# Two of four casts moved from VectorE to ScalarE, with reordered steps, in a fused recurrent-and-feed-forward kernel

## The chip, the cores and the metric

The kernel runs on one core of one Trainium2 chip. The metric is the device time of one execution in microseconds; of several runs the median is taken. Times inside an execution come from a profile of one run and count from the start of its span.

## The reference

The input x has 8 sequences of 512 positions with 128 features, in float32. Three residual stages follow each other:

```
x = x + 0.5 * ffn(layernorm(x))
x = x + attn(layernorm(x))
x = x + 0.5 * ffn(layernorm(x))      # the same weights as the first
ffn:  h = silu(x @ w1.T * s1) * (x @ w2.T * s2)       # 128 -> 512
      h = gelu(h @ h1.T * s3); h = gelu(h @ h2.T * s4) # 512 -> 512, twice
      return h @ w3.T * s5                             # 512 -> 128
attn: h_t = tanh(x_t @ B + h_(t-1) @ A.T)              # 16 states, along the sequence
      y = h @ C;  return y @ W_out.T + b_out
```

The middle stage is a scan along the 512 positions. The kernel cuts each sequence into 8 blocks of 64 positions, starts every block from a guess, and repeats the scan if the block ends disagree.

## The kernel before

**Tiles and turns.** The work is cut into 8 chunks of 512 columns (N), features or hidden units on the 128 partitions. Each chunk goes through the feed-forward stage twice, so there are 16 turns, g = 0 to 15. One turn computes, for its chunk, layer 2, layer 3 and layer 4 and, for the next chunk, layer 1. Layer 1 gives the product y1, layers 2 and 3 give y2 and y3, each with four tiles m = 0 to 3 of 128 hidden units. There are five kinds of turns: the first (g = 0), `early_turn` (g = 1 to 5), `middle_turn` (g = 6 to 8), `turn` with a next chunk (g = 9 to 14) and the last one (g = 15).

**Exactness.** Every activation is split in a high part, which is the value cast to the reduced type that TensorE multiplies, and a low part, value minus high part. Each product is then two matmuls of 128x128 by 512, one with each part (L256). The high part is made by a cast or, for y2 and y3, by a second Gelu straight from the accumulator (L1022, after L1019 has made the full value). The low part is a subtraction, on VectorE (`low`, L702) or on GpSimd (L1249).

**Layer 1 in pieces.** For each tile m, ScalarE makes tanh of the first product (`layer1`, th, L1001), VectorE makes u from it (`gate`, L675) and y1 from u and the second product (`gated`, L685), and VectorE then casts y1 into y1_hi (`y1_high`, L692). For chunk 0 alone ScalarE casts y1 (L1006). GpSimd makes y1_lo of tiles 0 to 2, VectorE that of tile 3. One semaphore, y1_hi_r, counts all casts: tile m of chunk g is there at 4g + m + 1.

**The scan.** It goes beside the feed-forward work, eight steps in a turn. One step is a chain over three engines: TensorE multiplies the last state by A (a matmul with 32 columns, L388), ScalarE makes two tanh of 32 columns (L1038, L1039), and VectorE subtracts to get the mixed state h (`scan_low`, L721). TensorE's next step waits for that. The first pass of the scan goes in turns 2 to 6, the second in turns 6 to 13.

**Order.** Every engine has one queue in program order, and the order of all work on it is written out by hand in the turn functions. A wait holds all that is behind it on its engine. TensorE's order in a turn is layer 2 of tiles 0 to 3 (with layer 4 of the chunk before, the attention product and the front transposes set into tile 0), layer 1 of the next chunk's tiles 0 and 1, layer 3 of tile 0, layer 1 of tile 2, layer 3 of tiles 1 and 2, layer 1 of tile 3, layer 3 of tile 3, with `scan_step` set between. In early turns steps 3, 6 and 7 stand in front of layer 1 tile 0, layer 3 tile 2 and layer 1 tile 3. In middle turns the second-pass steps stand two to a tile of layer 3.

**Normalisation.** In early turns the chunk g + 2 is normalised with tokens on the partitions: VectorE takes statistics (`first_stats`) and the negated mean (`mean_negated`, nmean), GpSimd makes the inverse deviation (rs_f, L1244) and the bias (nbias, L1259), and ScalarE applies them in four instructions of 128 columns (`normalise`, L1056). Chunk `mid` = g - 1 is normalised for the scan on VectorE, after `middle_stats`. From turn 7 on, the front of the next chunk comes from the attention result: VectorE adds the residual into lnin (L729), TensorE transposes it (`front_tokens`, L274), VectorE takes statistics.

The lines that ScalarE runs in an early turn, and VectorE's order around the casts:

```
gelu2(g, 1, lambda: step(1))
normalise(g + 2)
step(2)
...
gate(g, 0); step(at[0]); gated(g, 0); gate(g, 1); y1_high(g, 0); step(at[1])
gated(g, 1); step(at[2]); y1_high(g, 1); gate(g, 2); step(at[3])
gated(g, 2); step(at[4]); y1_high(g, 2)
```

Of the kernel before, what the change touches and what calls it, by code (L numbers as in the profile page):

```python
# [35 lines left out]
CHUNKS = 8  # L36
# [20 lines left out]
def build(nc, xT, xtok, w1T, w2T, h1T, h2T, w3T, scales, Ablk, Brep, CTrep, WoutT, ident_d, mask_d, outT):  # L57
    with ExitStack() as ctx:
# [129 lines left out]
        th_r = sem("th_r")  # L188
        u_r = sem("u_r")
        y1_r = sem("y1_r")  # L190
        y1_hi_r = sem("y1_hi_r")
        y1_lo_pool = sem("y1_lo_pool")
        y1_lo_dve = sem("y1_lo_dve")
        l2_mm = sem("l2_mm")
# [56 lines left out]
        def _(pe):  # L251
# [71 lines left out]
            def layer2(g, m, gen, beside=lambda k: None):  # L323
                if m == 0:
                    pe.wait_ge(y1_r, 4 * g + 3)
                if m == 1:
                    wait(pe, y3_hi_r, 4 * g)
                if m == 2:
                    wait(pe, l4_out, g)
                for k in range(KT):  # L330
                    if m == 0:
                        pe.wait_ge(y1_hi_r, 4 * g + k + 1)
                        if k < KT - 1:
                            pe.wait_ge(y1_lo_pool, (KT - 1) * g + k + 1)
# [96 lines left out]
            def first_layer2(m, ks, gen, high=True, finish=False):  # L431

                for k in ks:
                    if high:
                        pe.wait_ge(y1_hi_r, k + 1)
                        if k < KT - 1:
                            pe.wait_ge(y1_lo_pool, k + 1)
                        else:
                            pe.wait_ge(y1_lo_dve, 1)
                    mm = split_mm(B2[m][:, :], 2, k, m, y1_hi[:, k, :], y1_lo[:, k, :], high and k == 0,  # L440
                                  finish and k == KT - 1, gen, high)
                if finish:
                    mm.then_inc(l2_mm, 1)
# [183 lines left out]
        def _(dve):  # L627
# [61 lines left out]
            def y1_high(g, m):  # L689
                dve.wait_ge(y1_r, 4 * g + m + 1)  # L690
                wait(dve, l2_mm, 4 * g)
                nc.vector.tensor_copy(y1_hi[:, m, :], y1[:, m, :]).then_inc(y1_hi_r, 1)  # L692

            def layer1(g, m, late=False):
                gate(g, m, late)
                gated(g, m, late)
                if not late and not (isinstance(g, int) and g == 0):
                    y1_high(g, m)

            def low(g, k, hi_r, y, y_hi, y_lo, out_sem):  # L700
                dve.wait_ge(hi_r, 4 * g + k + 1)
# [51 lines left out]
            def first_gates(g, step, at):  # L753

                gate(g, 0)
                step(at[0])
                gated(g, 0)
                gate(g, 1)
                y1_high(g, 0)
                step(at[1])  # L760
                gated(g, 1)
                step(at[2])
                y1_high(g, 1)
                gate(g, 2)
                step(at[3])
                gated(g, 2)
                step(at[4])
                y1_high(g, 2)

            def end_turn(g):  # L770

                gated(g + 1, KT - 1)
                y1_high(g + 1, KT - 1)
                low(g + 1, KT - 1, y1_hi_r, y1, y1_hi, y1_lo, y1_lo_dve)
                low(g, 3, y3_hi_r, y23, y3_hi, y3_lo, y3_lo_dve)

            def early_turn(g, mid, scan):
                def step(t):
                    if scan is not None and t is not None:
                        scan_low(scan, t)  # L780
                xn_low(g + 1)
                layer4(0, g - 1, g - 1)
                step(0)
                first_stats(g + 2)
                middle_stats(mid)
                mean_negated(g + 2)
                step(1)
                low(g, 1, y2_hi_r, y23, y2_hi, y2_lo, y2_lo_dve)
                step(2)
                normalise("m", mid, MI, mv_m, rs_m, xnt_m)  # L790
                step(3)
                low(g, 3, y2_hi_r, y23, y2_hi, y2_lo, y2_lo_dve)
                first_gates(g + 1, step, (4, None, 5, None, None))
                step(6)
                low(g, 1, y3_hi_r, y23, y3_hi, y3_lo, y3_lo_dve)
                step(7)
                low(g, 2, y3_hi_r, y23, y3_hi, y3_lo, y3_lo_dve)
                gate(g + 1, KT - 1)
                end_turn(g)

            def middle_turn(g, c):
# [31 lines left out]
                    xn_low(g + 1)  # L833
                    normalise("m", mid, MI, mv_m, rs_m, xnt_m)
                low(g, 3, y2_hi_r, y23, y2_hi, y2_lo, y2_lo_dve)
                first_gates(g + 1, step, (None, 0, 1, 2, 3))
                step(4)
                low(g, 1, y3_hi_r, y23, y3_hi, y3_lo, y3_lo_dve)
                step(5)
# [6 lines left out]
            def turn(k, g, att, scan, joined=True):  # L846
# [19 lines left out]
                step(3)  # L866
                low(g, 3, y2_hi_r, y23, y2_hi, y2_lo, y2_lo_dve)
                if not last:
                    first_gates(g + 1, step, (4, None, 5, None, None))
                step(6)  # L870
                low(g, 1, y3_hi_r, y23, y3_hi, y3_lo, y3_lo_dve)
                step(7)
# [50 lines left out]
            nc.vector.tensor_scalar(general[:, :], F[4][0:1, 0:1], 0.0, None, ALU.is_gt).then_inc(gen_ready, 1)  # L923

            xn_low(1)
            low(0, KT - 1, y1_hi_r, y1, y1_hi, y1_lo, y1_lo_dve)
            first_stats(2)
            mean_negated(2)
            low(0, 1, y2_hi_r, y23, y2_hi, y2_lo, y2_lo_dve)
            low(0, 3, y2_hi_r, y23, y2_hi, y2_lo, y2_lo_dve)  # L930
            for m in range(KT - 1):
                layer1(1, m)
            low(0, 1, y3_hi_r, y23, y3_hi, y3_lo, y3_lo_dve)
            low(0, 2, y3_hi_r, y23, y3_hi, y3_lo, y3_lo_dve)
            layer1(1, KT - 1)
            low(0, 3, y3_hi_r, y23, y3_hi, y3_lo, y3_lo_dve)
            low(1, KT - 1, y1_hi_r, y1, y1_hi, y1_lo, y1_lo_dve)
            early_turn(1, 0, None)
            early_turn(2, 1, 0)
            with dve.Fori(3, FIRST_PASS + 1) as k:  # L940
# [4 lines left out]
            def round_(r):  # L945
                gb = r * CHUNKS
                if isinstance(r, int):
                    middle_turn(CHUNKS, 2)
                else:
                    restart(r)  # L950
                    for t in range(CSTEPS):
                        scan_low(gb + FIRST_PASS, t)
                    attention(gb, 0)
                    front_stats(gb + CHUNKS)
                    normalise("f", gb + CHUNKS, FR, mv_f, rs_f, xnt_f)
                    for t in range(CSTEPS):
                        scan_low(gb + FIRST_PASS + 1, t)
                    xn_low(gb + CHUNKS)
                    attention(gb + 1, 1)
                    for m in range(KT):  # L960
                        layer1(gb + CHUNKS, m, late=True)
                    low(gb + CHUNKS, KT - 1, y1_hi_r, y1, y1_hi, y1_lo, y1_lo_dve)
                    turn(0, gb + CHUNKS, None, gb + FIRST_PASS + 2, False)
                turn(1, gb + 1 + CHUNKS, (gb + 2, 2), gb + FIRST_PASS + 3)
                with dve.Fori(2, CHUNKS - 2) as k:
# [25 lines left out]
        def _(act):  # L991
# [11 lines left out]
            def y1_high(g, m):  # L1003
                act.wait_ge(y1_r, 4 * g + m + 1)
                wait(act, l2_mm, 4 * g)
                nc.scalar.copy(y1_hi[:, m, :], y1[:, m, :]).then_inc(y1_hi_r, 1)  # L1006

            def layer1_late(g, beside=lambda m: None):
                for m in range(KT):
# [39 lines left out]
                act.wait_ge(step_h, n * CSTEPS)  # L1049
                nc.scalar.copy(SC[:, 0:HCOLS], cols(xb_all, c, HCOLS)).then_inc(sc_set, 1)  # L1050

            def normalise(g):
                act.wait_ge(nbias_r, g)
                wait(act, feat["f"], g)
                for q in range(QT):
                    i = nc.scalar.activation(xnt_f[:, q * P:(q + 1) * P], cols(xt_all, g)[:, q * P:(q + 1) * P],  # L1056
                                             ACT.Identity, bias=nbias[:, q:q + 1], scale=rs_f[:, q:q + 1])
                i.then_inc(normed["f"], 1)

            def early_turn(g, mid, scan):  # L1060
# [3 lines left out]
                step(0)  # L1064
                gelu2(g, 0)
                gelu2(g, 1, lambda: step(1))
                normalise(g + 2)
                step(2)
                gelu2(g, 2)
                step(3)  # L1070
                gelu2(g, 3)
# [3 lines left out]
                middle_copy(mid)  # L1075
                step(5)
                gelu3(g, 0, lambda: layer1(g + 1, 2))
                step(6)
                gelu3(g, 1)
                step(7)  # L1080
                gelu3(g, 2)
                layer1(g + 1, 3)
                gelu3(g, 3)
                front(g + 2)
                keep_xb(mid)

            def middle_turn(g, c):
                mid = g - 1
# [18 lines left out]
                middle_copy(mid)  # L1107
                keep_xb(mid)
                step(0)
                gelu3(g, 0, lambda: layer1(g + 1, 2))  # L1110
                step(1)
                step(2)
                step(3)
                gelu3(g, 1, lambda: step(4))
                step(5)
                gelu3(g, 2, lambda: step(6))
                layer1(g + 1, 3)
                step(7)
# [2 lines left out]
            def turn(g, nxt, scan):  # L1121
# [16 lines left out]
                step(4)  # L1138
                step(5)
                gelu3(g, 0, lambda: layer1(g + 1, 2) if nxt else None)  # L1140
                step(6)
                gelu3(g, 1)
                step(7)
                gelu3(g, 2)
                if nxt:
# [47 lines left out]
            gelu2(0, 3)  # L1193
            layer1(1, 1)
            layer1(1, 2)
            gelu3(0, 0)
            gelu3(0, 1)
            gelu3(0, 2)
            layer1(1, 3)
            gelu3(0, 3)  # L1200
# [37 lines left out]
        def _(pool):  # L1238
            def inverse_std(kind, g, mv, ve, rs):
# [3 lines left out]
                wait(pool, normed[kind], g)  # L1243
                pool.tensor_tensor(rs[:, :], ve[:, :], mhalf[:, :], ALU.pow).then_inc(rstd[kind], 1)  # L1244

            def low(g, k, hi_r, per, y, y_hi, y_lo, out_sem, free):
                pool.wait_ge(hi_r, 4 * g + k + 1)
                wait(pool, *free)
# [1 line left out]

            def layer1(g, ms=range(KT - 1)):
                for m in ms:
                    low(g, m, y1_hi_r, 4, y1, y1_hi, y1_lo, y1_lo_pool, (l2_mm, 4 * g))

            def bias(g):
                pool.wait_ge(rstd["f"], g + 1)
# [162 lines left out]
```

## Time and profile before

| What | Value |
|---|---|
| runs | 426.45, 427.07, 427.39 us; median 427.07 |
| profiled execution | 425.79 us |
| its span | 424.0 us, of which 1.8 us lie outside |
| TensorE matmuls busy | 392.3 us, 93% |
| VectorE busy | 298.5 us, 70% |
| ScalarE busy | 254.8 us, 60% |
| GpSimd busy | 165.8 us, 39% |
| TensorE clock granted over the span | 0.979 |

A busy share is the time in which an engine ran instructions, over the span. TensorE's matmuls overlap in the record, so a matmul that shows 0.40 us can be followed by the next after 0.23 us. A share of 93% says that TensorE sets the time in most places, and that the places where it stands are what other engines can give back.

### The profile page before, as it was taken

What the parts mean: (1) busy time and instruction counts of PE and PEld (TensorE: products, weight loads), DVE (VectorE), ACT (ScalarE), POOL (GpSimd) and SP (SyncE); (2) the same over time, 40 slices, a digit from 0 to 9 for tenths busy, and PEclk for the clock granted to TensorE, in tenths of its full rate; (3) what the DMA queues carried; (4) which work ended last, traced back from release to release, by engine and by line L of the source; (5) the groups of instructions that cost most, each with busy time, mean ns of one, the idle gap of its engine ahead of it and who ended that gap; (6) DMA issues with size and microseconds to landing.
All of it is one profiled execution on the core that took longest, in us unless ns stands there. A gap on an engine that the chain in (4) does not pass through costs nothing.

```text
span 424.0 us, 6711 instructions
## 1 busy us (share of the span) xinstructions
PE 392.3 (93%) x1787; PEld 301.2 (71%) x1787; DVE 298.5 (70%) x756; ACT 254.8 (60%) x609; POOL 165.8 (39%) x156
## 2 busy tenths in 40 slices
PE   6868999999999999998989989999999999999981
PEld 4655877777777777776767767777877777777760
DVE  4694869687676859577787876878678685877511
ACT  3547576575758657676555666656565766656550
POOL 3334455461535535153351533525233353525120
PEclk9698999999999999999999999999999999999996
DMA  7900000000000000000101001010100001010001
GB/s 256 424 16 2 1 26 0 26 2 25 2 1 25 0 25 0 25 2 1 49 2 49 2 0 52 1 49 2 49 0 25 25 0 49 0 50 2 25 1 32
DMA packets 6078, 14.02 MB, mean 33 GB/s; under 512 B 1056, under 2 KB 1568, under 8 KB 5792
## 3 DMA queue, kind: packets, MB, share of 16 engines
q1 hardware_dynamic: 5040, 13.37, 8.2%
q10 hardware_dynamic: 1008, 0.29, 0.3%
q8 instruction: 13, 0.21, 0.2%
q14 instruction: 17, 0.14, 0.1%
HBM read 7.37 MB, written 2.10 MB: 22 GB/s over the span
## 4 chain that ended last, share of the span: by engine, by line
PE 52%; issue 16%; DVE 15%; ACT 10%; POOL 3%; DMA 1%; DVEq 1%; ACTq 0%; POOLq 0%
PE F L256 44%; DVE u L675 5%; DVE y L685 3%; ACT th L1001 2%; ACT y_hi L1022 2%; ACT xnt_f L1056 2%; PE FR L284 2%; ACT y L1019 2%; DVE xnt_f L663 1%; POOL rs_f L1244 1%; DVE y_hi L692 1%; PE SC L373 1%; DVE st_f L630 1%; PE SC L388 1%; DVE h L721 1%
## 5 line engine op out<-in xcount | busy, mean ns | idle before, releaser
L256 PE MATMUL F<-y_hi,w_hi 128*128 128x512 f32 x512 | 211.9, 414 | 7.4 <-DVE y_lo L702 2.5
L256 PE MATMUL F<-y_lo,w_hi 128*128 128x512 f32 x512 | 203.0, 396 | 0.0
L1249 POOL TENSOR_TENSOR y_lo<-y,y_hi 128x512 fp32r<-128x512 f32 x96 | 130.2, 1363 | 105.7 <-DVE y_hi L692 60.2
L256 PEld LDWEIGHTS F<-y_hi,w_hi 128*128 128x128 f32 x512 | 96.5, 189 | 33.9 <-issue 5.9
L256 PEld LDWEIGHTS F<-y_lo,w_hi 128*128 128x128 f32 x512 | 96.8, 189 | 18.4
L1019 ACT ACTIVATE y<-F,sc 128x512 f32<-128x512 f32 x112 | 76.5, 683 | 51.2 <-PE F L256 51.2
L702 DVE TENSOR_TENSOR y_lo<-y,y_hi 128x512 fp32r<-128x512 f32 x96 | 68.8, 729 | 44.4 <-ACT y_hi L1022 44.0
L1022 ACT ACTIVATE y_hi<-F,sc 128x512 fp32r<-128x512 f32 x112 | 76.4, 682 | 0.0
L1038 ACT ACTIVATE h<-SC 128x32 fp32r<-128x32 f32 x104 | 20.3, 195 | 77.2 <-PE SC L388 77.2
L256 PE MATMUL F<-xn_hi,w_hi 128*128 128x512 f32 x119 | 50.7, 426 | 2.2 <-POOL w_lo L1295 1.9
L1241 POOL TENSOR_TENSOR ve_f<-mv_f,epsc 128x4 f32<-128x4 f32 x16 | 3.2, 200 | 114.1 <-DVE mv_f L635 108.8
L256 PE MATMUL F<-xn_lo,w_hi 128*128 128x512 f32 x119 | 47.2, 396 | 0.0
L692 DVE CAST y_hi<-y 128x512 fp32r<-128x512 f32 x60 | 45.6, 760 | 1.1
L1001 ACT ACTIVATE th<-F,s1h 128x512 f32<-128x512 f32 x61 | 40.7, 688 | 7.4 <-PE F L256 5.2
L685 DVE SCALAR_TENSOR_TENSOR y<-F,s12h,u 128x512 f32<-128x512 f32 x58 | 43.4, 748 | 1.8
L675 DVE SCALAR_TENSOR_TENSOR u<-th,F 128x512 f32<-128x512 f32 x61 | 41.4, 678 | 2.2 <-ACT th L1001 2.2
L721 DVE TENSOR_TENSOR h<-SC,h 64x32 fp32r<-64x32 f32 x104 | 18.4, 177 | 29.8 <-ACT SC L1039 29.0
L388 PEld LDWEIGHTS SC<-h,a_mix 128*128 128x128 f32 x103 | 19.3, 187 | 21.1 <-DVE h L721 17.7
L256 PEld LDWEIGHTS F<-xn_hi,w_hi 128*128 128x128 f32 x119 | 22.6, 190 | 8.8 <-ACT w_hi L1152 2.1
L388 PE MATMUL SC<-h,a_mix 128*128 128x32 f32 x103 | 20.9, 203 | 8.3 <-DVE h L721 8.3
L256 PE MATMUL FR<-y_hi,w_hi 128*128 128x512 f32 x64 | 26.0, 406 | 0.6 <-DVE y L685 0.6
L256 PE MATMUL FR<-y_lo,w_hi 128*128 128x512 f32 x64 | 25.3, 395 | 0.0
(121 smaller groups left out, 359.0 us busy)
## 6 DMA issues: line engine op xcount, KB each, us to landing
x_all<-in_xT SPq DMA_DIRECT2D x1, 2048.0 KB, 16.7
x_all<-x1c SPq DMA_DIRECT2D x8, 256.0 KB, 2.3
x_all<-lnin SPq DMA_DIRECT2D x8, 256.0 KB, 2.3
out<-outb SPq DMA_DIRECT2D x8, 256.0 KB, 2.1
x_all<-in_xtok SPq DMA_DIRECT2D x1, 1536.0 KB, 12.5
w_raw<-in_h1T SPq DMA_DIRECT2D x2, 512.0 KB, 7.7
w_raw<-in_h2T SPq DMA_DIRECT2D x2, 512.0 KB, 9.5
x_all<-in_xtok SPq DMA_DIRECT2D x2, 256.0 KB, 4.6
```

The costliest lines, as they stand in the source:

```text
L256: mm = nc.tensor.matmul(out, wtile(w, layer, k, m), y, start=first and i == 0, stop=last and i == len(pairs) - 1)
L388: nc.tensor.matmul(SC[:, span(t)], a_mix[:, :], states, start=False, stop=True, skip_group_check=True).then_inc(step_mm, 1)
L675: nc.vector.scalar_tensor_tensor(out=u[:, m % 2, :], in0=th[:, m % 2, :], scalar=1.0, in1=l1_banks(g, m, late)[0][:, :], op0=ALU.add, op1= ...
L685: nc.vector.scalar_tensor_tensor(out=y1[:, m, :], in0=l1_banks(g, m, late)[1][:, :], scalar=s12h[:, m:m + 1], in1=u[:, m % 2, :], op0=ALU. ...
L692: nc.vector.tensor_copy(y1_hi[:, m, :], y1[:, m, :]).then_inc(y1_hi_r, 1)
L702: nc.vector.tensor_tensor(y_lo[:, k, :], y[:, k, :], y_hi[:, k, :].bitcast(F32), ALU.subtract).then_inc(out_sem, 1)
L721: nc.vector.tensor_tensor(h[0:64, span(t)], SC[0:64, span(CSTEPS + t)], h[0:64, span(t)].bitcast(F32), ALU.subtract).then_inc(step_h, 1)
L1001: nc.scalar.activation(th[:, m % 2, :], l1_banks(g, m, late)[0][:, :], ACT.Tanh, scale=s1h[:, m:m + 1]).then_inc(th_r, 1)
L1019: nc.scalar.activation(y23[:, m, :], bankt[:, :], ACT.Gelu, scale=s)
L1022: nc.scalar.activation(y_hi[:, m, :], bankt[:, :], ACT.Gelu, scale=s).then_inc(hi_r, 1)
L1038: nc.scalar.activation(h[:, span(t)], SC[:, span(t)], ACT.Tanh)
L1249: pool.tensor_tensor(y_lo[:, k, :], y[:, k, :], y_hi[:, k, :].bitcast(F32), ALU.subtract).then_inc(out_sem, 1)
```

## The change

ScalarE takes over the casts of y1's tiles 1 and 2 for every chunk from 1 on; tiles 0 and 3 stay on VectorE. Since two engines now cast, each tile gets a semaphore of its own, y1_hi_r[m], and the waits on TensorE, VectorE and GpSimd name the tile. In early turns scan step 2 on ScalarE goes between the second and the third of the four `normalise` instructions, and the negated mean goes ahead of `middle_stats` on VectorE. In middle turns scan step 1 on ScalarE goes ahead of the tanh of tile 2, and a cast stands behind step 2 and another behind step 5. No matmul, no DMA and no arithmetic is added or removed.

```diff
-        y1_hi_r = sem("y1_hi_r")
+        y1_hi_r = [sem(f"y1_hi_r{m}") for m in range(KT)]
...
-                        pe.wait_ge(y1_hi_r, 4 * g + k + 1)
+                        pe.wait_ge(y1_hi_r[k], g + 1)
...
             def layer1(g, m, late=False):            # VectorE
                 gate(g, m, late)
                 gated(g, m, late)
-                if not late and not (isinstance(g, int) and g == 0):
-                    y1_high(g, m)
+
+            def low1(g):
+                dve.wait_ge(y1_hi_r[KT - 1], g + 1)
+                nc.vector.tensor_tensor(y1_lo[:, KT - 1, :], y1[:, KT - 1, :], y1_hi[:, KT - 1, :].bitcast(F32),
+                                        ALU.subtract).then_inc(y1_lo_dve, 1)
...
                 gated(g, 1)                           # VectorE, first_gates
                 step(at[2])
-                y1_high(g, 1)
                 gate(g, 2)
                 step(at[3])
                 gated(g, 2)
-                step(at[4])
-                y1_high(g, 2)
...
                 first_stats(g + 2)                    # VectorE, early_turn
+                mean_negated(g + 2)
                 middle_stats(mid)
-                mean_negated(g + 2)
...
-            def normalise(g):                         # ScalarE
+            def normalise(g, between=lambda: None):
                 act.wait_ge(nbias_r, g)
                 wait(act, feat["f"], g)
                 for q in range(QT):
+                    if q == QT // 2:
+                        between()
...
-                normalise(g + 2)                      # ScalarE, early_turn
-                step(2)
+                normalise(g + 2, lambda: step(2))
...
                 gelu3(g, 0, lambda: layer1(g + 1, 2))
+                y1_high(g + 1, 1)
                 step(6)
                 gelu3(g, 1)
+                y1_high(g + 1, 2)
                 step(7)
...
+            def first_and_gate(g, step):
+                step(1)
+                layer1(g + 1, 2)
...
                 step(0)                               # ScalarE, middle_turn
-                gelu3(g, 0, lambda: layer1(g + 1, 2))
-                step(1)
+                gelu3(g, 0, lambda: first_and_gate(g, step))
                 step(2)
+                y1_high(g + 1, 1)
                 step(3)
                 gelu3(g, 1, lambda: step(4))
                 step(5)
+                y1_high(g + 1, 2)
                 gelu3(g, 2, lambda: step(6))
...
                 gelu3(g, 0, lambda: layer1(g + 1, 2) if nxt else None)   # ScalarE, turn
+                if nxt:
+                    y1_high(g + 1, 1)
                 step(6)
                 gelu3(g, 1)
+                if nxt:
+                    y1_high(g + 1, 2)
                 step(7)
```

In `middle_turn` and `turn` VectorE's order stays as it was without the two casts. The first turn gets the same two casts on ScalarE, between the two Gelus of layer 3 tiles 0 and 1. GpSimd's `low1` is the same subtraction as before with the tile's own semaphore.

## Rows read from the trace of the kernel before

**Rows 1.** Waits: engine and line, whom it waited for; total us, times, longest.
```profile
PE SC L388 <- DVE h L721: 8.3, 19, 0.7
```
**Rows 2.** Timeline of TensorE, early turn 5: start, us, instruction, idle before.
```profile
158.18 0.40 PE L256 MATMUL F<-y_lo,w_hi 128*128 128x512 f32 x1
...
159.35 0.50 PE L256 MATMUL F<-xn_hi,w_hi 128*128 128x512 f32 x1
...
163.68 0.48 PE L256 MATMUL F<-xn_hi,w_hi 128*128 128x512 f32 x1
...
166.55 0.18 PE L388 MATMUL SC<-h,a_mix 128*128 128x32 f32 x1
166.77 0.50 PE L256 MATMUL F<-y_hi,w_hi 128*128 128x512 f32 x1
...
168.50 0.40 PE L256 MATMUL F<-y_lo,w_hi 128*128 128x512 f32 x1
...
169.40 0.47 PE L256 MATMUL F<-xn_hi,w_hi 128*128 128x512 f32 x1
```
**Rows 3.** Timeline of GpSimd, ScalarE and VectorE in early turn 5, normalisation and first gate.
```profile
154.52 1.01 POOL L1244 TENSOR_TENSOR rs_f<-ve_f,mhalf 128x4 f32<-128x4 f32 x1 [0.16 <-POOL ve_f L1241]
156.15 0.61 POOL L1259 TENSOR_TENSOR nbias<-nmean,rs_f 128x4 f32<-128x4 f32 x1 [0.62 <-POOL rs_f L1244]
...
156.99 1.65 ACT L1056 ACTIVATE xnt_f<-x_all,nbias,rs_f 128x128 f32 x4 [1.27 <-POOL nbias L1259]
...
162.78 0.75 DVE L685 SCALAR_TENSOR_TENSOR y<-F,s12h,u 128x512 f32<-128x512 f32 x1
```
**Rows 4.** Timeline of GpSimd, VectorE and ScalarE in early turn 5, around the cast of tile 2.
```profile
166.22 2.54 POOL L1249 TENSOR_TENSOR y_lo<-y,y_hi 128x512 fp32r<-128x512 f32 x2 [0.39 <-ACT y_hi L1022]
...
167.62 1.43 DVE L692 CAST y_hi<-y 128x512 fp32r<-128x512 f32 x1
...
167.53 0.68 ACT L1022 ACTIVATE y_hi<-FR,sc 128x512 fp32r<-128x512 f32 x1
```
**Rows 5.** The two cast lines by source: count, shortest/median/longest ns, first and last start.
```profile
L692 DVE CAST y_hi<-y x60: 408/428/1503, 40.6 to 394.6; 128x512 fp32r<-128x512 f32 x60
L1006 ACT CAST y_hi<-y x4: 617/623/627, 17.3 to 26.5; 128x512 fp32r<-128x512 f32 x4
```
**Rows 6.** Timeline of TensorE and VectorE, middle turn 7 and opening of turn 8.
```profile
217.12 0.40 PE L256 MATMUL FR<-y_lo,w_hi 128*128 128x512 f32 x1
...
218.33 0.48 PE L256 MATMUL FR<-y_hi,w_hi 128*128 128x512 f32 x1
...
219.12 0.40 PE L256 MATMUL FR<-y_lo,w_hi 128*128 128x512 f32 x1
...
220.30 0.48 PE L256 MATMUL F<-y_hi,w_hi 128*128 128x512 f32 x1
...
228.36 0.75 DVE L729 SCALAR_TENSOR_TENSOR lnin<-MI,sc,x_all 128x512 f32<-128x512 f32 x1
...
229.16 0.66 PE L274 MATMUL FR<-ident,lnin 128*128 128x128 f32 x4
```
**Rows 7.** Timeline of TensorE and VectorE, turn 11 and opening of turn 12.
```profile
317.44 0.18 PE L388 MATMUL SC<-h,a_mix 128*128 128x32 f32 x1
317.73 0.50 PE L256 MATMUL F<-y_hi,w_hi 128*128 128x512 f32 x1
...
319.46 0.40 PE L256 MATMUL F<-y_lo,w_hi 128*128 128x512 f32 x1
...
320.28 0.48 PE L256 MATMUL F<-xn_hi,w_hi 128*128 128x512 f32 x1
...
325.63 0.74 DVE L729 SCALAR_TENSOR_TENSOR lnin<-MI,sc,x_all 128x512 f32<-128x512 f32 x1
...
326.70 0.65 PE L274 MATMUL FR<-ident,lnin 128*128 128x128 f32 x4
```
**Rows 8.** Timeline of TensorE in early turn 1, which has no scan.
```profile
60.70 0.50 PE L256 MATMUL F<-xn_hi,w_hi 128*128 128x512 f32 x1 [0.27 <-ACT y_hi L1022]
```

More of the change, by code:

```diff
@@ L434, in first_layer2 @@
                     if high:
-                        pe.wait_ge(y1_hi_r, k + 1)
+                        pe.wait_ge(y1_hi_r[k], 1)
                         if k < KT - 1:
@@ L691, in y1_high @@
                 wait(dve, l2_mm, 4 * g)
-                nc.vector.tensor_copy(y1_hi[:, m, :], y1[:, m, :]).then_inc(y1_hi_r, 1)
+                nc.vector.tensor_copy(y1_hi[:, m, :], y1[:, m, :]).then_inc(y1_hi_r[m], 1)
             def layer1(g, m, late=False):
@@ L773, in end_turn @@
                 y1_high(g + 1, KT - 1)
-                low(g + 1, KT - 1, y1_hi_r, y1, y1_hi, y1_lo, y1_lo_dve)
+                low1(g + 1)
                 low(g, 3, y3_hi_r, y23, y3_hi, y3_lo, y3_lo_dve)
@@ L792, in early_turn @@
                 low(g, 3, y2_hi_r, y23, y2_hi, y2_lo, y2_lo_dve)
-                first_gates(g + 1, step, (4, None, 5, None, None))
+                first_gates(g + 1, step, (4, None, 5, None))
                 step(6)
@@ L835, in middle_turn @@
                 low(g, 3, y2_hi_r, y23, y2_hi, y2_lo, y2_lo_dve)
-                first_gates(g + 1, step, (None, 0, 1, 2, 3))
+                first_gates(g + 1, step, (None, 0, 1, 2))
+                step(3)
                 step(4)
@@ L868, in turn @@
                 if not last:
-                    first_gates(g + 1, step, (4, None, 5, None, None))
+                    first_gates(g + 1, step, (4, None, 5, None))
                 step(6)
@@ L925, in _ @@
             xn_low(1)
-            low(0, KT - 1, y1_hi_r, y1, y1_hi, y1_lo, y1_lo_dve)
+            low1(0)
             first_stats(2)
@@ L932, in _ @@
                 layer1(1, m)
+                if m == 0:
+                    y1_high(1, 0)
             low(0, 1, y3_hi_r, y23, y3_hi, y3_lo, y3_lo_dve)
@@ L935, in _ @@
             layer1(1, KT - 1)
+            y1_high(1, KT - 1)
             low(0, 3, y3_hi_r, y23, y3_hi, y3_lo, y3_lo_dve)
-            low(1, KT - 1, y1_hi_r, y1, y1_hi, y1_lo, y1_lo_dve)
+            low1(1)
             early_turn(1, 0, None)
@@ L961, in round_ @@
                         layer1(gb + CHUNKS, m, late=True)
-                    low(gb + CHUNKS, KT - 1, y1_hi_r, y1, y1_hi, y1_lo, y1_lo_dve)
+                    low1(gb + CHUNKS)
                     turn(0, gb + CHUNKS, None, gb + FIRST_PASS + 2, False)
@@ L1005, in y1_high @@
                 wait(act, l2_mm, 4 * g)
-                nc.scalar.copy(y1_hi[:, m, :], y1[:, m, :]).then_inc(y1_hi_r, 1)
+                nc.scalar.copy(y1_hi[:, m, :], y1[:, m, :]).then_inc(y1_hi_r[m], 1)
             def layer1_late(g, beside=lambda m: None):
@@ L1195, in _ @@
             layer1(1, 2)
-            gelu3(0, 0)
-            gelu3(0, 1)
+            gelu3(0, 0, lambda: y1_high(1, 1))
+            gelu3(0, 1, lambda: y1_high(1, 2))
             gelu3(0, 2)
@@ L1244, in inverse_std, with low1 @@
                 pool.tensor_tensor(rs[:, :], ve[:, :], mhalf[:, :], ALU.pow).then_inc(rstd[kind], 1)
+            def low1(g, m):
+                pool.wait_ge(y1_hi_r[m], g + 1)
+                wait(pool, l2_mm, 4 * g)
+                pool.tensor_tensor(y1_lo[:, m, :], y1[:, m, :], y1_hi[:, m, :].bitcast(F32),
+                                   ALU.subtract).then_inc(y1_lo_pool, 1)
             def low(g, k, hi_r, per, y, y_hi, y_lo, out_sem, free):
@@ L1252, in layer1 @@
                 for m in ms:
-                    low(g, m, y1_hi_r, 4, y1, y1_hi, y1_lo, y1_lo_pool, (l2_mm, 4 * g))
+                    low1(g, m)
             def bias(g):
```

## The prediction

> **What bounds the kernel now.** I read the waits first, then TensorE's timeline turn by turn, then the other engines around each gap. The first part of the page has TensorE nearly always busy, so time can only come from places where it stands. The largest wait of its matmuls after the start is for VectorE's scan state: 8.3 us in 19 waits [rows 1]. They fall two to a scanning early turn (g = 2 to 5), two to a middle turn (6 to 8), one to each of turns 9 to 13.
>
> The idle figure is less than what a gap costs, so I count from start to start. Between the first matmul of layer 1 tile 2 and scan step 6 of turn 5 lie 12 large matmuls in 2.87 us, 0.24 us each [rows 2]; a scan matmul that waits for nothing adds 0.03 us. What exceeds 0.24 or 0.27 us is a gap. Early turn 5 has three [rows 2]: 1.17 - 0.27 = 0.90 us at step 3, 0.22 - 0.03 = 0.19 us behind step 6, 0.90 - 0.27 = 0.63 us at step 7. A middle turn has two, 1.21 - 0.27 = 0.94 us at step 2 and 1.18 - 0.27 = 0.91 us at step 4 [rows 6]. A late turn has 0.29 - 0.03 = 0.26 us behind step 6 and 0.82 - 0.27 = 0.55 us at step 7 [rows 7].
>
> Two causes stand behind them. VectorE's cast takes 0.43 us alone, but up to 1.50 us [rows 5]. The long ones are those beside GpSimd: GpSimd's pair of subtractions ends at 168.76 us, and the cast that began at 167.62 us ends at 169.05 us, 0.29 us later [rows 4]. The cast stood until GpSimd was through, and scan steps and the gate of tile 2 stood behind it. The other cause is ScalarE: step 2 of an early turn waits behind a normalisation of 1.65 us, which itself began late because the bias waited for the negated mean [rows 3], and step 1 of a middle turn waits behind a tanh and a Gelu of tile 0.
>
> **The change part by part.**
>
> Casts. VectorE loses 30 of its 60 casts, ScalarE gets 30 of about 0.62 us [rows 5]. On VectorE the cast of tile 1 stood ahead of the gate of tile 2, that of tile 2 ahead of step 6 (early and late turns). Both leave the path, so the gap behind step 6 and the gap at step 7 close. On ScalarE the casts stand in front of steps 6 and 7. In turn 5 y1 of tile 2 is complete by 167.62 us, when the old cast begins, and ScalarE is busy with the Gelu of tile 1 until 168.21 us [rows 4], so the cast does not wait for its input. The step behind it starts when TensorE's matmul arrives, which is about when the cast ends; I cost it at nothing there, at most 0.62 us of delay for whoever is next on ScalarE.
>
> Semaphores per tile. The same waits with other names, no instruction more: nothing, in either direction, since each wait asks for the same cast as before.
>
> Negated mean first. VectorE stands before the middle statistics anyway, so this one short instruction of four columns is covered by TensorE's transposes. The bias then follows rs_f: it waited 0.62 us, and a hand-over inside GpSimd takes 0.16 us [rows 3]; it starts 0.46 us earlier. If the bias were not what ScalarE waits for, the gain would be 0; it is named as the releaser, so I take 0.46 (ends 0 and 0.62).
>
> Step 2 between halves. It begins behind 0.82 us of normalisation instead of 1.65 us, so with the bias it is 1.29 us earlier, more than the 0.90 us of the gap at step 3: that wait is gone. What is late next is the rest of ScalarE's queue. The Gelus of tiles 2 and 3 come only 0.46 us earlier, and through them VectorE's y1 of tile 0, for which TensorE's layer 1 tile 2 waits. That y1 ends at 163.53 us, TensorE starts at 163.68 us [rows 2, 3]; with 0.05 us of hand-over (as lnin to transpose, [rows 6]) 0.10 us are spare. So of the 0.90 us, 0.46 + 0.10 = 0.56 us can be kept, and I take 0.55.
>
> Early turns 2 to 5: 0.55 + 0.19 + 0.63 = 1.37 us each, 5.5 us (ends: 0.90 in place of 0.55 gives 6.9; 0.10 gives 3.7). Turn 1 has no scan, but TensorE waits there for a Gelu behind the same normalisation [rows 8]; 0.5 us, and 0.26 us as behind step 6: 0.76 us (0.27 to 0.9). The first turn has its casts where TensorE waits for tile 1's y1 itself: nothing.
>
> Middle turns. ScalarE's step 1 no longer waits for tanh and Gelu, so step 2 on TensorE comes in time. VectorE's step 3 stood behind the gate of tile 2, which stood behind a long cast; without it step 4 is in time. I walked the order through with the durations of the rows: tanh, Gelu and cast now stand between steps 1, 2 and 3 on ScalarE, and about 0.05 us is lost there. The larger debt comes due in the next turn. ScalarE has 1.24 us more to do between the third-layer Gelus, VectorE's gate of tile 3 falls back by about 0.34 us against TensorE, and VectorE is then busy without a break until lnin. lnin ends at 229.11 us and the transpose starts at 229.16 us [rows 6], nothing spare. So 0.94 + 0.91 - 0.05 - 0.34 = 1.46 us each, 4.4 us for three (ends: 1.85, and 0.6 if both casts are due in full, hence 5.6 and 1.8).
>
> Turns 9 to 13: 0.26 + 0.55 = 0.81 us. The same debt arises, because VectorE's subtraction of tile 2 now meets GpSimd's last one, but here at most 326.70 - 0.05 - 326.37 = 0.28 us are spare at the transpose [rows 7]. Lateness I estimate as in the middle turns, 0.34 to 0.4 us, of which 0.10 us is left: 0.71 us each, 3.55 us for five (ends 4.05 and 1.0). Turn 14 has no scan and keeps 0.26 us.
>
> Sum: 5.5 + 0.76 + 4.4 + 3.55 + 0.26 = 14.5 us. The profiled execution took 425.79 us, so 411.3 us; it lies 1.28 us under the median of the runs, so the median goes from 427.07 to 412.6 us. All gaps closed without debt would be 17.5 us, 409.5 us.
>
> A rule speaks against the move. The row shows the cast at 0.43 us on VectorE alone and 0.62 us on ScalarE [rows 5], so ScalarE is dearer wherever GpSimd is quiet. The Trainium skill (Perfetto Trace Analysis, Optimizing Scalar/DVE Operations) says that an operation which has a VectorE performance mode is faster there, and that moving it to ScalarE may make sense if VectorE is saturated. VectorE is at 70% and not saturated. By that rule 30 casts would each cost about 0.2 us more, some 6 us if all lie on the path, and eat two fifths of the gain; the long casts of the row are what speaks for the move all the same.
>
> **The rivals.**
>
> *ScalarE becomes the link that is late.* Every cast lies in the queue between two scan steps. If the 0.19 us by which it is dearer is on the path in all 30 cases, that is 5.7 us: 412.6 + 5.7 = 418.3 us. Nearly the same comes out if in middle turns the four steps 1 to 4 are each 0.3 us late (3.6 us for three turns) and the early bias brings nothing (0.46 us in five turns, 2.3 us). For it: the queue of a middle turn has little air. Against it: ScalarE waited for TensorE's scan step in most places. The rule cited above points here. Chance 0.17.
>
> *Slower: ScalarE stands at the cast.* The queue is in order. If y1 of tile 2 came after the Gelu of tile 1, ScalarE would stand with step 7, two Gelus and the tanh of tile 3 behind it, and the opening of the next turn would be late. It decides from the point where the loss of a turn exceeds its gain, 14.5 / 14, about 1.0 us; the spare time in turn 5 is 168.21 - 167.62 = 0.6 us and grows since VectorE is relieved, so y1 would have to be 1.6 us later than now. If it were 2.1 us later, 0.5 us net in 14 turns give 434 us. The rows speak against it. Chance 0.05.
>
> *It does not do what it says.* The gaps close but TensorE waits as long somewhere else, the tiles' low parts for instance, which GpSimd now gets in another rhythm; 427 us. The low parts of tiles 1 and 2 are needed only in the next turn, which speaks against it. Chance 0.04.
>
> **How the numbers follow.** The forecast as summed has chance 0.74, with 409.5 to 416 us as its own range (the ends of the terms do not all fall together). About 0.2%, 0.9 us, is what a measurement of this kernel can tell from no change. The first rival is faster too, so faster has 0.74 + 0.17, and same and slower take 0.04 and 0.05. The range from 409.5 to 418.0 us takes in the forecast and a part of the first rival.
>
> **What would show it right or wrong.** In the profile after, the wait of L388 for VectorE falls from 8.3 us to under 2 us and from 19 to a few. Line 692 has 30 casts near 0.43 us and the casts on ScalarE are 34 at 0.62 us. Early turns fall by about 1.4 us, middle ones by 1.5, late ones by 0.7. In early turns layer 1 tile 2 shows a new small wait for y1, and behind middle turns the transpose of lnin shows one of 0.3 us. If the ScalarE casts took over 0.8 us, or if layer 2 waited for a low part of y1, the forecast would be wrong; if the wait of L388 stayed over 4 us, the first rival has it.

## The result and the profile after

The changed kernel takes 409.14 us (median of 4 runs, 408.61 to 409.59) against 426.76 us for the kernel before in the same comparison: a ratio of 0.960, 95% interval 0.958 to 0.963, or 17.6 us less. The forecast was 412.6 us, with a range from 409.5 to 418.0 us, worked out from a median of 427.07 us for the kernel before. The spans of the two profiled executions differ by 424.0 - 407.7 = 16.3 us.

First the head of the profile's page after, with the busy time of each engine, and the slices of TensorE:

```profile
span 407.7 us, 6683 instructions
PE 385.1 (94%) x1787; PEld 302.0 (74%) x1787; DVE 275.1 (67%) x726; ACT 270.4 (66%) x639; POOL 165.6 (41%) x156
...
PE   6868999999999999999999999999999999999980
```

VectorE lost 30 instructions and 23.4 us of busy time, ScalarE gained 30 and 15.6 us. TensorE ran the same 1787 matmuls. Next the two cast lines by source; they answer to [rows 5]:

```profile
L692 DVE CAST y_hi<-y x30: 411/426/429, 40.8 to 378.1; 128x512 fp32r<-128x512 f32 x30
L1010 ACT CAST y_hi<-y x34: 611/617/634, 17.5 to 373.6; 128x512 fp32r<-128x512 f32 x34
```

No cast on VectorE is long any more: the longest takes 429 ns instead of 1503. The waits of line 388, whose row before is [rows 1], show how little of the scan's hold is left. The matmul itself has no row any more, only its weight load. Here are the rows of ScalarE's wait for the scan matmul and of the weight load, first before, then after:

```profile
ACT h L1038 <- PE SC L388: 77.2, 76, 3.0
PEld SC L388 <- DVE h L721: 17.7, 24, 1.1
```

```profile
ACT h L1042 <- PE SC L388: 53.7, 53, 3.2
PEld SC L388 <- DVE h L724: 1.8, 8, 0.3
```

The time before TensorE's turns begin differs by up to 2.9 us from one profiled execution to the next, whatever the kernel. So I compare turns. A turn is taken from its opening transposes to those of the next, in us. Turns 1 to 7 go by those of L264, from turn 7 on by those of L274:

| From turn to turn | before | after | gain | forecast |
|---|---|---|---|---|
| 1 to 2 | 23.67 | 22.66 | 1.01 | 0.76 |
| 2 to 3 | 24.76 | 23.37 | 1.39 | 1.37 |
| 3 to 4 | 25.31 | 23.37 | 1.94 | 1.37 |
| 4 to 5 | 25.12 | 23.38 | 1.74 | 1.37 |
| 5 to 6 | 25.25 | 23.49 | 1.76 | 1.37 |
| 6 to 7 | 26.44 | 24.83 | 1.61 | 1.46 |
| 7 to 9, mean of two | 26.30 | 24.70 | 1.60 | 1.46 |
| 9 to 10 | 23.42 | 22.73 | 0.69 | 0.71 |
| 10 to 14, mean of four | 23.95 | 23.18 | 0.77 | 0.71 |

From the transposes of turn 1 to those of turn 14 it is 319.54 us before and 303.10 us after, 16.4 us less. This stretch is what I use to set the experiments beside each other. What follows it took 49.3 us before and 49.2 us after.

### The profile page after: what moved, and what is told of

Its sections match the earlier page's. It is cut to its first block, busy times and chain, and to the rows that moved or that the text cites. A ratio compares the mean times of both kernels' runs of the same rounds, so it can differ in the third digit from the quotient of the medians.

```text
span 407.7 us, 6683 instructions
## 1 busy us (share of the span) xinstructions
PE 385.1 (94%) x1787; PEld 302.0 (74%) x1787; DVE 275.1 (67%) x726; ACT 270.4 (66%) x639; POOL 165.6 (41%) x156
## 4 chain that ended last, share of the span: by engine, by line
PE 81%; DVE 7%; ACT 4%; issue 3%; POOL 2%; DMA 1%; DVEq 0%; POOLq 0%; ACTq 0%
PE F L256 67%; PE FR L256 8%; PE FR L284 2%; DVE xnt_f L663 1%; POOL rs_f L1260 1%; PE SC L373 1%; DVE st_f L630 1%; DVE u L675 1%; ACT y_hi L1026 1%; DVE y L685 1%; PE MI L284 1%; DMA x_all<-in_xtok 1%; PE MI L264 1%; ACT th L1005 1%; ACT y L1023 1%
## 5 line engine op out<-in xcount | busy, mean ns | idle before, releaser
L705 DVE TENSOR_TENSOR y_lo<-y,y_hi 128x512 fp32r<-128x512 f32 x80 | 65.0, 812 | 54.1 <-ACT y_hi L1026 54.1
L256 PEld LDWEIGHTS F<-xn_lo,w_hi 128*128 128x128 f32 x119 | 22.8, 191 | 3.5
L388 PEld LDWEIGHTS SC<-h,a_mix 128*128 128x128 f32 x103 | 19.3, 188 | 6.1 <-DVE h L724 1.8
```

The lines of the kernel that those rows point to most:

```text
L256: mm = nc.tensor.matmul(out, wtile(w, layer, k, m), y, start=first and i == 0, stop=last and i == len(pairs) - 1)
L388: nc.tensor.matmul(SC[:, span(t)], a_mix[:, :], states, start=False, stop=True, skip_group_check=True).then_inc(step_mm, 1)
L705: nc.vector.tensor_tensor(y_lo[:, k, :], y[:, k, :], y_hi[:, k, :].bitcast(F32), ALU.subtract).then_inc(out_sem, 1)
```

## Experiments

All are edits of the changed kernel. Each was measured against the kernel before on the same chip. The medians of the kernel before lay between 426.02 and 426.76 us.

**Casts only.** ScalarE casts, but no step is moved.

```diff
-                mean_negated(g + 2)
                 middle_stats(mid)
+                mean_negated(g + 2)
...
-                normalise(g + 2, lambda: step(2))
+                normalise(g + 2)
+                step(2)
...
-                gelu3(g, 0, lambda: first_and_gate(g, step))
+                gelu3(g, 0, lambda: layer1(g + 1, 2))
+                step(1)
                 step(2)
```

> Only the casts are moved; the negated mean, scan step 2 of early turns and scan step 1 of middle turns stand where they stood before. Theory A (the parts add up, gap by gap): the gaps behind step 6 and at step 7 close in early turns (0.19 + 0.63 us in four turns, 0.26 us in turn 1) and in late ones (0.8 us in five), and at step 4 in middle turns (0.9 us in three): about 10 us of the 17.6 us, 416.5 us. The gap at step 3 of early turns (0.9 us) and at step 2 of middle turns (0.94 us) stay. Theory B (the order is what counts, the casts only follow): under 5 us, above 421.5 us.

Measured: 415.04 us, ratio 0.973 (0.969 to 0.977); the stretch of turns took 309.44 us, 10.1 us less than before. That is theory A's figure. Late turns are as in the changed kernel (23.13 us). In early turns the wait behind step 6 and the one at step 7 are gone and the one at step 3 stays (0.79 us in turn 5, counted as in the prediction). In middle turns the gap at step 2 stays, as TensorE's timeline of turn 7 in this run shows (start, us, instruction, idle before):

```profile
212.62 0.40 PE L256 MATMUL FR<-y_lo,w_hi 128*128 128x512 f32 x1
213.70 0.28 PE L388 MATMUL SC<-h,a_mix 128*128 128x32 f32 x1 [0.68 <-DVE h L724]
213.83 0.48 PE L256 MATMUL FR<-y_hi,w_hi 128*128 128x512 f32 x1
```

From 212.62 to 213.83 us it is 1.21 us, the same as in [rows 6]. There is no second gap in the turn: with the cast off VectorE, step 4 is in time although step 2 is late.

**Order only.** The steps stay moved, VectorE casts in the old places.

```diff
                 gated(g, 1)
                 step(at[2])
+                y1_high(g, 1)
                 gate(g, 2)
                 step(at[3])
                 gated(g, 2)
+                step(at[4])
+                y1_high(g, 2)
```

(and the same two casts taken out of ScalarE's turns)

> All reordering is kept (negated mean, split normalisation, step 1 ahead of the tanh), but VectorE casts tiles 1 and 2 in their old places. Theory A: 0.9 us in four early turns, 0.5 us in turn 1, 0.94 us in three middle turns: about 7 us, 420 us; the long casts beside GpSimd and the gaps at step 7 remain. Theory B: 12 us or more, below 414.5 us.

Measured: 415.84 us, ratio 0.976 (0.972 to 0.980), the stretch 309.40 us, 10.1 us less. That is between the two theories, and 3 us more gain than A had. Late turns are as before within 0.07 us, early ones win 0.67 to 1.37 us. The difference to A's figure is in the middle turns. From turn 7 to turn 8 it took 24.54 us, less than the 24.70 us of the changed kernel, though VectorE still casts there. VectorE's and GpSimd's timelines of turn 7 show why:

```profile
207.95 0.17 DVE L724 TENSOR_TENSOR h<-SC,h 64x32 fp32r<-64x32 f32 x1
208.07 0.68 DVE L692 CAST y_hi<-y 128x512 fp32r<-128x512 f32 x1
208.66 0.68 DVE L675 SCALAR_TENSOR_TENSOR u<-th,F 128x512 f32<-128x512 f32 x1
...
207.16 1.29 POOL L1258 TENSOR_TENSOR y_lo<-y,y_hi 128x512 fp32r<-128x512 f32 x1 [2.94 <-DVE y_hi L692]
```

Scan step 1 comes earlier, so the cast of tile 1 starts 0.38 us before GpSimd's first subtraction ends (207.16 + 1.29 = 208.45 us) and takes 0.68 us, where it took 1.35 us in the kernel before. With the cast on VectorE, then, the gap at step 4 follows from the one at step 2; the casts-only run closes it the other way, by taking the cast off VectorE. Either edit is enough for that gap. The two sets of edits overlap: 10.1 + 10.1 = 20.2 us apart, 16.4 us together.

**Negated mean back** behind the middle statistics, all else as changed.

```diff
                 first_stats(g + 2)
-                mean_negated(g + 2)
                 middle_stats(mid)
+                mean_negated(g + 2)
```

> The changed kernel with the negated mean back behind the middle statistics. In the trace after, ScalarE starts to normalise 1.06 us sooner after the inverse deviation than before, not 0.46 us, because the bias also takes 0.20 us instead of 0.61 us. Theory A (the bias was held up by VectorE's subtraction of y2_lo at the shared port, besides starting late): the bias takes 0.6 us again, layer 1 waits in early turns, 0.8 us in four turns and 0.5 us in turn 1: 412.8 us. Rival (only the 0.46 us of the later start count): 0.35 us in five turns, 410.8 us.

Measured: 412.16 us, ratio 0.966 (0.962 to 0.970), the stretch 306.61 us. One short instruction in another place is worth 3.5 us, 0.7 us in each of turns 1 to 5. Here are GpSimd's and VectorE's rows of early turn 5 in this run, then GpSimd's and ScalarE's of the changed kernel:

```profile
150.80 1.01 POOL L1260 TENSOR_TENSOR rs_f<-ve_f,mhalf 128x4 f32<-128x4 f32 x1 [0.16 <-POOL ve_f L1257]
152.43 0.61 POOL L1281 TENSOR_TENSOR nbias<-nmean,rs_f 128x4 f32<-128x4 f32 x1 [0.63 <-POOL rs_f L1260]
...
152.16 0.14 DVE L653 TENSOR_SCALAR nmean<-mv_f 128x4 f32<-128x4 f32 x1
...
152.31 0.67 DVE L705 TENSOR_TENSOR y_lo<-y,y_hi 128x512 fp32r<-128x512 f32 x1
```

```profile
148.65 1.01 POOL L1260 TENSOR_TENSOR rs_f<-ve_f,mhalf 128x4 f32<-128x4 f32 x1 [0.16 <-DVE nmean L653]
149.74 0.20 POOL L1281 TENSOR_TENSOR nbias<-nmean,rs_f 128x4 f32<-128x4 f32 x1
...
150.06 0.88 ACT L1062 ACTIVATE xnt_f<-x_all,nbias,rs_f 128x128 f32 x2 [0.21 <-POOL nbias L1281]
```

With the mean late, the bias lands beside VectorE's subtraction of y2_lo and takes 0.61 us, until 153.04 us, 0.06 us after that subtraction ends (152.98 us). With the mean early it takes 0.20 us. That is so throughout: the median of the 7 instructions is 609 ns before and in this run, and 201 ns in the changed kernel. From the end of rs_f to the start of ScalarE's normalising it was 156.99 - 155.53 = 1.46 us before [rows 3], and is 150.06 - 149.66 = 0.40 us now.

TensorE's rows of early turn 5 in this run show where the time is lost:

```profile
154.47 0.39 PE L256 MATMUL F<-y_lo,w_hi 128*128 128x512 f32 x1
154.70 0.18 PE L388 MATMUL SC<-h,a_mix 128*128 128x32 f32 x1
154.76 0.49 PE L256 MATMUL F<-xn_hi,w_hi 128*128 128x512 f32 x1
...
155.55 0.40 PE L256 MATMUL F<-xn_lo,w_hi 128*128 128x512 f32 x1
156.18 0.50 PE L256 MATMUL F<-xn_hi,w_hi 128*128 128x512 f32 x1 [0.23 <-ACT y_hi L1026]
```

It is not lost at step 3: with the split and the late bias 0.29 us lie between the matmuls around the scan step, where 0.27 us is no gap. It is lost behind it: 156.18 - 155.55 - 0.24 = 0.39 us at layer 1 tile 1, which waits for a Gelu behind the late normalisation, and 159.77 - 159.33 - 0.27 = 0.17 us at layer 1 tile 2. The changed kernel has neither wait.

**No split.** Scan step 2 behind all four normalising instructions.

```diff
-                normalise(g + 2, lambda: step(2))
+                normalise(g + 2)
+                step(2)
```

> The changed kernel with scan step 2 behind all four normalising instructions. Theory A (with the early bias step 2 has time to spare: before it was due 0.9 us too late and it is now 1.06 us earlier): no difference, 409.1 us within 0.6. Rival (the split is needed): the gap at step 3 comes back with 0.4 us or more in four turns, 410.7 us or more.

Measured: 409.49 us, ratio 0.961 (0.957 to 0.965), the stretch 303.14 us against 303.10. The split is worth nothing once the bias is early. The run before shows the reverse for step 3: the split closes that gap also with a late bias. So either of the two closes it, but only the early bias brings the Gelus behind it in time.

**VectorE casts, but later** in its queue.

```diff
                 gate(g, 2)
+                y1_high(g, 1)
                 step(at[3])
                 gated(g, 2)
...
                 step(6)                               # step(4) in middle turns
+                y1_high(g + 1, 2)
                 low(g, 1, y3_hi_r, y23, y3_hi, y3_lo, y3_lo_dve)
```

(and ScalarE's two casts taken out of all turns)

> The changed kernel with the casts of tiles 1 and 2 on VectorE again, but not in their old places: that of tile 1 behind the gate of tile 2, that of tile 2 behind step 6 (behind step 4 in middle turns). Theory P (the place in VectorE's queue is what counted): the gaps stay closed and it takes 409 to 411 us. Theory L (the length counts too: a cast beside GpSimd's subtractions waits for the port and takes 1 to 1.5 us wherever it stands, and holds step 6 or the opening of the next turn): 0.3 to 0.7 us more in each of 9 early and late turns, 412 to 416 us.

Measured: 411.65 us, ratio 0.967 (0.963 to 0.971), the stretch 305.36 us, 2.3 us more than with ScalarE's casts. It lies between the theories. The place in the queue is worth most of it: early turns are as good as in the changed kernel but for one (3 to 4, 23.50 us), middle ones 0.1 us longer. Late turns take 23.46 us instead of 23.12 us, where VectorE's low parts of tiles 1 and 2, which stand in front of the residual add, take 1.53 and 1.24 us against 1.10 and 0.81 us in the same turn of the changed kernel:

```profile
304.70 1.53 DVE L705 TENSOR_TENSOR y_lo<-y,y_hi 128x512 fp32r<-128x512 f32 x1 [0.17 <-ACT y_hi L1030]
306.15 0.17 DVE L724 TENSOR_TENSOR h<-SC,h 64x32 fp32r<-64x32 f32 x1
306.69 1.24 DVE L705 TENSOR_TENSOR y_lo<-y,y_hi 128x512 fp32r<-128x512 f32 x1 [0.37 <-ACT y_hi L1030]
```

The length that theory L asked for did not come back: from turn 1 on one cast a turn is held up at all, and none takes more than 0.77 us, where up to two a turn took 0.96 to 1.50 us in the kernel before.

**Casts twice.**

```diff
+                if m in (1, 2) and not (isinstance(g, int) and g == 0):
+                    wait(act, dup_r, 2 * (g - 1))
+                    nc.scalar.copy(y1_dup[:, m - 1, :], y1[:, m, :]).then_inc(dup_r, 1)
                 nc.scalar.copy(y1_hi[:, m, :], y1[:, m, :]).then_inc(y1_hi_r[m], 1)
```

> The changed kernel with each of ScalarE's 30 casts done twice, first into a tile that nobody reads; the output is the same. Theory A (ScalarE has next to nothing spare behind the cast of tile 2, since VectorE's work up to lnin hangs on its next Gelu): two casts of 0.57 us more, about 0.9 us in each of turns 6 to 13 and little in early turns, where the opening has slack: 7 us more, 416 us. Rival (ScalarE, busy 66%, has room): under 2 us more, below 411 us.

Measured: 413.98 us, ratio 0.971 (0.968 to 0.975). The first cast of a pair takes 0.51 us from start to start, 30 of them 15 us, and 4.8 us of it show in the medians, 4.3 us in the stretch. Early turns do not change at all (23.37 and 23.38 us). From turn 7 to 8 it goes from 24.70 to 25.42 us, from 11 to 12 from 23.11 to 23.52 us. So theory A has the right turns and about one and a half times the size; ScalarE's spare time is neither none nor plenty, but differs by stage.

**Transposes later.**

```diff
-                if not last:
-                    to_features("f", xnt_f, FR, g + 1)
-                layer2(g, 3, gen)
+                layer2(g, 3, gen, lambda k: to_features("f", xnt_f, FR, g + 1) if k == 0 and not last else None)
```

> The changed kernel with one further step on TensorE in turns 9 to 14: the transposes back to features stand behind the first two matmuls of layer 2 tile 3 instead of ahead of them. In the trace after, they wait 0.37 us for VectorE's normalised tile in four turns. If that wait is covered by the two matmuls (0.47 us), layer 1 of the next chunk still has its input in time and it takes 1.5 us less than the changed kernel, 407.6 us. If ScalarE's copy and VectorE's low part behind the transposes are late for layer 1 instead, the same 409.1 us.

Measured: 409.34 us, ratio 0.961 (0.957 to 0.964). No gain; the wait only moved. TensorE's rows, first of the changed kernel at the transposes of turn 11, then of this run at layer 1 of the same turn:

```profile
293.82 0.18 PE L388 MATMUL SC<-h,a_mix 128*128 128x32 f32 x1
294.21 0.44 PE L284 MATMUL FR<-ident,xnt_f 128*128 128x128 f32 x2 [0.21 <-DVE xnt_f L663]
```

```profile
295.13 0.18 PE L388 MATMUL SC<-h,a_mix 128*128 128x32 f32 x1
295.55 0.49 PE L256 MATMUL F<-xn_hi,w_hi 128*128 128x512 f32 x1 [0.24 <-DVE xn_lo L668]
```

**Middle casts on VectorE**, in their old places, with the new order of steps.

```diff
                 step(at[2])
+                if cast:
+                    y1_high(g, 1)
                 gate(g, 2)
...
-                first_gates(g + 1, step, (None, 0, 1, 2))
+                first_gates(g + 1, step, (None, 0, 1, 2), True)
                 step(3)
+                y1_high(g + 1, 2)
                 step(4)
```

(and the same two casts taken out of ScalarE's middle turns)

> The changed kernel with the two casts of middle turns alone back on VectorE, in their old places; the order of steps is kept. In the run with order only a middle turn took 24.54 us from turn 7 to turn 8, in the changed kernel 24.70 us. If the order of steps alone closed the gaps of middle turns and ScalarE's casts cost something there: 0.16 us less in three turns, 408.6 us. If both are needed in middle turns: 2.7 us more, 411.8 us, as I forecast when I put the gap at step 4 down to the long cast.

Measured: 408.78 us, ratio 0.958 (0.953 to 0.962). A median of 0.4 us below the changed kernel is within the spread of the runs, but the turns are plain: 24.55 us from turn 7 to turn 8 instead of 24.70 us, the stretch 302.58 us instead of 303.10 us. The casts on ScalarE cost a little in middle turns, about 0.15 us a turn; that rests on the turns of the profiled executions, not on the medians.

**Statistics first** in turns 9 to 14.

```diff
-                if joined:
-                    layer4(1, g - 1, k - 1)
                 if not last:
                     front_stats(g + 1)
                 step(0)
+                if joined:
+                    layer4(1, g - 1, k - 1)
                 step(1)
```

> The changed kernel with VectorE's front statistics and scan step 0 of turns 9 to 14 ahead of the layer 4 output instead of behind it. The run with the transposes later showed that in these turns the chain from lnin over statistics, inverse deviation, normalising, transposes and low part to layer 1 is due 0.4 us too late wherever the transposes stand. The output of 0.75 us on VectorE stands in that chain. Theory A (this chain is the bound): the statistics start about 0.4 us sooner, the wait of 0.37 us at the transposes goes in five turns, 1.5 to 1.8 us less than the changed kernel, 407.5 us. Rival (layer 2 tile 2 then waits for the output that frees its accumulator): no gain, 409.1 us.

Measured: 407.73 us, ratio 0.956 (0.953 to 0.959), the stretch 302.01 us against 303.10. The wait for VectorE's tile is gone, and turns 10 to 13 take 22.84 us instead of 23.12 us, 13 to 14 takes 23.10 us instead of 23.35 us. The gain is 1.1 us, less than the 1.5 us expected: turn 9 to 10 did not change (22.72 us).

**Both of them.**

> The same with the casts of middle turns on VectorE as well. If the two gains are in different turns they add: 0.16 us in three turns more, 407.0 us; lower than every other kernel here.

Measured: 407.69 us, ratio 0.957 (0.955 to 0.959). In the stretch the gains add, 301.51 us; the medians do not tell this run from the one before it. Either is below the changed kernel by about 1.4 us, and below the kernel before by more than 18 us.

## Why the prediction was right, and where it was not

The direction and most of the size were right, and the main mechanism held: TensorE's gaps at the scan steps closed, without a new one of the same size. The time sits at the very edge of the stated range. The median of 409.14 us is 0.4 us under its lower end of 409.5 us; but the kernel before came out at 426.76 us in this comparison, not at 427.07 us, and the ratio of 0.960 applied to 427.07 us gives 410.1 us, just inside. The gain was under-estimated, by 3 us in the medians and 1.8 us in the spans. By the turns, early ones gave 7.8 us where 6.2 were forecast, middle ones 4.8 for 4.4, late ones 3.8 for 3.55.

*Casts.* Right in early and late turns. With the casts moved alone, early turns 2 to 5 win 0.81 to 1.04 us where 0.19 + 0.63 = 0.82 us were forecast, late turns have their whole gain, and the cast takes 617 ns on ScalarE as costed. The step that "the cast does not wait for its input" held too.

*The bias.* This is the term that was mis-sized. I had it start 0.46 us earlier and took its own time as fixed. In turn 5 it starts 0.54 us earlier after the inverse deviation, takes 0.20 us instead of 0.61 us, because it no longer meets VectorE's subtraction, and ScalarE follows it 0.11 us sooner: ScalarE starts 1.06 us sooner instead of 0.46 us. I had named the port as the reason for the long casts and did not look at GpSimd's other instructions for the same mark, though the row of the bias ends 0.07 us after that subtraction in the kernel before as well (156.76 and 156.69 us). With 1.06 us the Gelus come early enough, so that the wait of layer 1 tile 2 that was to eat 0.35 us of the 0.90 us never arose: the profile after has none in the early turns, and they gave 1.74 to 1.94 us instead of 1.37 us in turns 3 to 5. With the mean put back that wait is there (0.17 us), and a larger one of 0.39 us at layer 1 tile 1, which the prediction did not have at all.

*Step 2 between halves.* Forecast, together with the bias, as what closes the gap at step 3. Without the split the gap stays closed, and with the split but a late bias it is closed as well. The prediction added up the 0.46 us of the bias and the 0.83 us of the split and compared only the sum with 0.90 us. Measured, each is enough alone, and what is left of the gain hangs on the bias.

*Middle turns.* The sum was near, its parts were not. I put the gap at step 4 down to the long cast. Moving the cast closes it, but the order alone does too, since the cast then starts ahead of GpSimd's next subtraction; so the moved cast adds nothing there. Of the 1.85 us of gaps 1.60 us were kept, so 0.25 us was lost where I had taken 0.39 us. TensorE's rows of the changed kernel in the opening of turn 8 show one delay of 0.16 us at layer 4's last tile and none at the transposes (218.33 us, after a matmul that began at 218.07 us):

```profile
217.36 0.39 PE L256 MATMUL F<-y_lo,w_hi 128*128 128x512 f32 x1
217.76 0.48 PE L256 MATMUL F<-y_hi,w_hi 128*128 128x512 f32 x1
218.07 0.39 PE L256 MATMUL F<-y_lo,w_hi 128*128 128x512 f32 x1
...
216.93 0.69 DVE L705 TENSOR_TENSOR y_lo<-y,y_hi 128x512 fp32r<-128x512 f32 x1
```

Counted from the first of TensorE's starts to the last it is 0.71 us for two matmuls that take 0.47 us undisturbed, 0.24 us in all, which is about the whole loss. The profile names no releaser here; by the times it is VectorE's last low part, which ends at 217.62 us, directly ahead of lnin. So the debt of VectorE is the one forecast, smaller, and it falls due at the matmul before the transposes.

*Late turns.* 0.77 us a turn for 0.71. The lateness against TensorE's opening is there, as 0.04 us instead of 0.10 us. The low part of tile 1 did meet GpSimd:

```profile
305.14 1.10 DVE L705 TENSOR_TENSOR y_lo<-y,y_hi 128x512 fp32r<-128x512 f32 x1 [0.96 <-ACT y_hi L1026]
...
304.40 2.99 POOL L1265 TENSOR_TENSOR y_lo<-y,y_hi 128x512 fp32r<-128x512 f32 x2
```

It got in between two of GpSimd's subtractions, and those two took 2.99 us where a pair undisturbed takes 2.54 us [rows 4]. The 0.26 us that turn 14 was to keep are there: from its transposes to the last matmul it is 40.17 us before and 39.87 us after. What follows the last matmul took 0.23 us longer, which is why the last stretch shows 49.3 and 49.2 us; why it did is open.

*The rule on ScalarE.* The sentence of the Trainium skill (Perfetto Trace Analysis, Optimizing Scalar/DVE Operations) that VectorE is the faster engine for such an operation agrees with the trace, 426 ns against 617 ns on ScalarE; its advice to move work when VectorE is saturated would have misled on the decision. ScalarE has room in early turns (its casts done twice cost nothing there), some in late turns (0.41 us lost for 1.02 us more work), and in middle turns (0.7 us lost) the casts are better on VectorE. Neither ScalarE's share of 66% after nor VectorE's of 70% before tells that.

*The rivals.* ScalarE as the late link: its sign was a wait of L388 over 4 us, and none is left; what its casts cost in middle turns is the 0.24 us a turn above at most. The slower one: in the whole trace ScalarE stood at a cast for its input three times, at the casts of chunk 0 before 27 us, which ScalarE had in the kernel before too; never at a moved one. The one of no gain: TensorE's matmuls waited 4.0 us for low parts before and 4.2 us after, so but for those 0.24 us the time did not come back there.

## What to carry to other kernels

A short instruction that a shared port holds up looks like a long one; compare each duration with its fastest of the same kind before taking it as fixed, on both sides of the port. Where several edits aim at the same gap, ask which of them alone closes it: here one moved instruction of four columns made the split of the normalisation worthless, and one moved scan step made the moved casts of the middle turns unnecessary. An edit that closes a gap can still leave its gain behind: the split alone closed the gap at step 3, and the time was lost at the next two tiles. And a wait that is covered by other work on the waiting engine moves to the next consumer, unless the chain in front of it is made shorter.

## What the runs showed of the hardware

GpSimd's 128x4 multiply (the bias) took 0.20 us alone and 0.61 us when it began beside a VectorE subtraction with two inputs in SBUF, and ended 0.06 us after it. The wait goes both ways: a VectorE cast ended 0.29 us after the GpSimd subtraction that it met [rows 4], another, in the run with order only, 0.30 us after. Between two subtractions that GpSimd has ready, VectorE gets its turn: in turn 11 of the changed kernel a subtraction that takes 0.69 us alone took 1.10 us and was done at 306.24 us, while GpSimd's pair lasted until 307.39 us. The Trainium skill (SBUF — State Buffer, SBUF: two separate sides) has the pair of ports as an exclusive lock that whichever starts first holds for the whole instruction; the trace agrees with that, in both directions, and adds that the lock is given up between instructions.
